# A fused selective-scan layer and mixture-of-experts layer on one core: five activation-table loads a step in place of seven, transposes in one pass, layer-norm statistics of two tiles in one operation, and new orders on four engines

## What is computed

```python
def s6(x):                                   # 32 x 256 x 128 -> the same
    u, o = split(x @ W_in.T)                 # 256 channels each
    u = silu(causal_conv4(u) + conv_b)       # depthwise, 4 taps
    g = u @ W_gate.T                         # 64 delta rows, 16 b, 16 c
    delta = softplus(g[..., :64] @ W_delta.T + delta_bias)
    A = -exp(A_log)                          # 256 channels x 16 states
    # over the positions t:
    h = exp(A * delta[t]) * h + (delta[t] * u[t]) * b[t]
    y[t] = sum_over_states(h * c[t]) + D * u[t]
    return (y * silu(o)) @ W_out.T

def ffn(x):                                  # 8 experts of width 176, the best 2 of them; 1 shared of 352
    scores = softmax(x @ gate_w.T)
    combine = top2(scores) / (sum_of_top2 + 1e-20) * 2.5
    routed = combine-weighted sum of (silu(x @ w_gate[e]) * (x @ w_up[e])) @ w_down[e]
    return routed + (silu(x @ sw_gate) * (x @ sw_up)) @ sw_down

x = x + s6(layernorm(x));  x = x + ffn(layernorm(x))
```

## Time and profile before

| what | value |
|---|---|
| median of three runs | 1169.36 us (1168.85 to 1170.06) |
| the profiled execution, its span | 1170.17 us, 1168.5 us |
| busy: TensorE matmuls, VectorE, ScalarE, GpSimd | 1090.4, 1063.1, 1081.4, 1067.8 us (93, 91, 93, 91%) |
| inject and read on GpSimd | 256 of 2389 ns, 192 of 2388 ns |
| scans on VectorE | 192 of 2284 ns, 64 of 2269 ns |
| decays on ScalarE | 1024 of 463 ns |
| table loads on ScalarE | seven lines of 31 to 35, and nine single ones, 1283 ns each |
| granted TensorE clock | 0.974 over the span |

### The profile page before, as it was taken

The page is one execution under the profiler, slowest core; times in us unless marked ns, Lnnn a source line. Parts: engine busy times, 40 slices in busy tenths (PEclk is TensorE's granted clock), DMA queues, the critical chain, the costliest instruction groups (busy, mean ns, idle before and its releaser), DMA issues.

```text
span 1168.5 us, 25617 instructions
## 1 busy us (share of the span) xinstructions
PE 1090.4 (93%) x9075; PEld 925.3 (79%) x9075; DVE 1063.1 (91%) x1702; ACT 1081.4 (93%) x2182; POOL 1067.8 (91%) x502
## 2 busy tenths in 40 slices
PE   5667999999999999999999999999999999998898
PEld 4435888888888888888888888888888888887687
DVE  5577999999999999999999999999999999998974
ACT  6888999999999999999999999999999999998763
POOL 3699999999999999999999999999999999999930
PEclk9677999999999999999999999999999999998999
DMA  6344444333444433344444334444433344443000
GB/s 173 109 114 110 115 101 102 94 84 107 115 115 101 115 90 88 92 115 114 118 103 101 87 87 111 115 115 102 102 98 85 101 114 115 99 106 99 9 5 10
DMA packets 71481, 115.05 MB, mean 98 GB/s; under 512 B 8173, under 2 KB 30394, under 8 KB 71354
## 3 DMA queue, kind: packets, MB, share of 16 engines
q1 hardware_dynamic: 71354, 113.42, 37.7%
HBM read 41.04 MB, written 5.24 MB: 40 GB/s over the span
## 4 chain that ended last, share of the span: by engine, by line
ACT 60%; issue 14%; POOL 9%; DVE 9%; PE 6%; DMA 1%; ACTq 0%; DVEq 0%; POOLq 0%
ACT decay_ps L538 26%; ACT g_silu L525 5%; DVE decay_ps L758 5%; POOL inject L440 5%; POOL read L454 4%; ACT L655 3%; ACT L642 3%; ACT L638 3%; ACT L692 3%; ACT L668 3%; ACT xn L559 2%; ACT xn L567 2%; DVE features L780 2%; PE acc_ps L1174 2%; ACT L648 2%
## 5 line engine op out<-in xcount | busy, mean ns | idle before, releaser
L440 POOL TENSOR_TENSOR inject<-rep,bc 128x1024 f32<-128x1024 f32 x256 | 605.6, 2389 | 6.3 <-DMA rep<-dd 6.2
L454 POOL TENSOR_TENSOR read<-state,bc 128x1024 f32<-128x1024 f32 x192 | 456.7, 2388 | 29.1 <-DVE state L758 28.9
L758 DVE TENSOR_TENSOR_SCAN state<-decay_ps,inject 128x1024 f32<-128x1024 f32 x192 | 438.6, 2284 | 28.2 <-ACT decay_ps L538 27.3
L538 ACT ACTIVATE decay_ps<-rep,neg_a 128x255 f32<-128x255 f32 x1024 | 425.8, 463 | 2.9 <-DVE state L758 2.5
L1174 PE MATMUL acc_ps<-ffn_down,features 128*128 128x128 f32 (+1 forms) x1792 | 268.3, 279 | 0.4 <-DVE features L788 0.3
L1174 PEld LDWEIGHTS acc_ps<-ffn_down,features 128*128 128x128 f32 (+1 forms) x1792 | 235.1, 191 | 29.6 <-issue 24.9
L1137 PE MATMUL work_ps<-xn2T_part,ffn_gate 128*128 128x256 f32 x1344 | 213.5, 295 | 3.0 <-DVE dd L838 0.7
L1146 PE MATMUL work_ps<-xn2T_part,ffn_up 128*128 128x256 f32 x1344 | 206.7, 293 | 10.1 <-ACT g_silu L525 8.6
L1137 PEld LDWEIGHTS work_ps<-xn2T_part,ffn_gate 128*128 128x128 f32 x1344 | 175.7, 191 | 33.7 <-DVE dd L838 16.5
L1146 PEld LDWEIGHTS work_ps<-xn2T_part,ffn_up 128*128 128x128 f32 x1344 | 172.6, 189 | 33.5 <-ACT xnT_part L579 14.4
L780 DVE TENSOR_TENSOR features<-g_silu,work_ps 128x512 f32<-128x512 f32 x224 | 153.4, 686 | 11.2 <-PE work_ps L1146 10.7
(11 more groups left out here) (143 smaller groups left out, 1316.0 us busy)
## 6 DMA issues: line engine op xcount, KB each, us to landing
rep<-dd SPq DMA_DIRECT2D x256, 256.0 KB, 4.7
bc<-bc_rows SPq DMA_DIRECT2D x64, 512.0 KB, 4.0
x_in<-in_L_attn_x_dram SPq DMA_DIRECT2D x32, 128.0 KB, 2.2
out_dram<-result SPq DMA_DIRECT2D x32, 128.0 KB, 1.8
bc_rows<-g_sb SPq DMA_DIRECT2D x32, 32.0 KB
state<-in_L_ffn_w_gate_dram SPq DMA_DIRECT2D x1, 704.0 KB, 4.3
inject<-in_L_ffn_w_up_dram SPq DMA_DIRECT2D x1, 704.0 KB, 6.0
ffn_down<-in_L_ffn_w_down_dram SPq DMA_DIRECT2D x1, 704.0 KB, 7.5
```

The source lines that it names most:

```text
L440: pool.tensor_tensor(inject[:, slot:slot + many], du_all, b_all, ALU.mult).then_inc(inject_done, many)
L454: pool.tensor_tensor(read[:, slot:slot + many], state[:, first:first + many], c_all, ALU.mult).then_inc(read_done, many)
L538: last = act.activation(decay_ps[:, at % 2, j, 1:T], rep[(HALVES * n + half) % RP][:, j, 0, 1:T], ACT.Exp, scale=neg_a[:, col:col + 1])
L758: dve.tensor_tensor_scan(to, decays, inject[:, at % RI].rearrange("p j t -> p (j t)"), 0.0, ALU.mult, ALU.add).then_inc(state_done, 1)
```

## The change

ScalarE's list is put in another order, with five loads in a step. The exponentials of the router and decays 1 go behind decays 0, into the same table set as before the step's end; norm1 goes from the end of a step to the start of the next, between the silus. The load ahead of the first log_vars now stands at the program's start, and three loads of the prologue go. The two statistics become one bn_stats each, which reads the two tiles alternately (element by element) so that its even and odd halves are the tiles; bn_aggr is dropped, and the log takes the sum of squares with a factor 1/128. The two turns of a normalised tile become transposes. PSUM banks are given out anew, and the orders on GpSimd, VectorE and TensorE change. SP's list stays. The line numbers of the changed program are lower by 3 to 30.

```diff
 
-GATE_BANK = [2, 0, 0, 1, 0, 1, 2]
-UP_BANK = [1, 2, 0, 1, 0, 0, 2]
-
-COMB_BANK = [1, 1, 0, 2, 0, 2]
+GATE_BANK = [2, 0, 0, 1, 0, 1, 1]
+UP_BANK = [1, 2, 1, 2, 0, 2, 1]
+
+COMB_BANK = [0, 1, 0, 2, 1, 0]
 
...
         x_in = [sb(f"x_in{i}", [P, TILES, DIM]) for i in range(RX)]
-        stats1 = sb("stats1", [P, TILES, 6])
-        stats2 = sb("stats2", [P, TILES, 6])
-        mean_var = sb("mean_var", [P, 2 * TILES, 2])
+        stats = sb("stats", [P, 2, 6])
...
+                    act.wait_ge(ln1_var, m + 5)
                 if m >= 0:
-                    act.wait_ge(ln2_var, TILES * (m + 1))
-                act.activation(log_var[:], mean_var[:, :, 1], ACT.Ln, bias=eps[:, 0:1]).then_inc(ln_small, 1)
-                act.activation(neg_mean[:], mean_var[:, :, 0], ACT.Copy, scale=-1.0).then_inc(ln_small, 1)
+                    act.wait_ge(ln2_var, m + 1)
+                act.activation(log_var[:], moments[:, :, 2], ACT.Ln, scale=1.0 / DIM, bias=eps[:, 0:1]).then_inc(ln_small, 1)
+                act.activation(neg_mean[:], moments[:, :, 1], ACT.Copy, scale=-1.0).then_inc(ln_small, 1)
 
             def rstds(m):
...
                 if on(-2):
+                    router_exps(k - 2)
+                if on(-2) or on(1):
                     act.preload_act_table_set("silu_and_others")
+                if on(-2):
                     silu(k - 2, 0)
                     silu(k - 2, 1)
-                if on(-2) or later(0):
-                    act.preload_act_table_set("natural_log_exp_and_others")
-                if on(-2):
-                    router_exps(k - 2)
-                if later(0):
-                    decays(k, 1)
-                if on(-2) or on(1):
-                    act.preload_act_table_set("silu_and_others")
+                if later(2):
+                    norm1(k + 2)
                 if on(-2):
...
                     act.preload_act_table_set("softplus")
-                if on(-2):
-                    act.wait_ge(h_done, PAIRS * (k - 2) + 4)
-                if on(2) and not on(-2):
-                    act.wait_ge(xnT_low, k + 3)
+                if on(-1):
+                    act.wait_ge(x1_done, k)
+                if on(-2) and not on(-1):
+                    act.wait_ge(h_done, PAIRS * (k - 2) + 3)
...
                 if later(2):
                     copy_z(k + 2)
                 if later(1):
                     decays(k + 1, 0)
-
+                    decays(k + 1, 1)
+
+            act.preload_act_table_set("natural_log_exp_and_others")
             log_vars(-4)
             rstds(-4)
-            act.preload_act_table_set("silu_and_others")
             norm1(0)
             xn_high(0)
             xn_low(0)
...
-                dve.wait_ge(ln1_var, TILES * n)
-                for j in range(TILES):
-                    last = dve.bn_stats(stats1[:, j, :], x_in[n % RX][:, j, :])
-                last.then_inc(stats1_done, 1)
-
-            def moments_x(n):
-                dve.wait_ge(stats1_done, n + 1)
                 dve.wait_ge(ln_small, 2 * n)
-                for j in range(TILES):
-                    dve.bn_aggr(mean_var[:, j, :], stats1[:, j, :]).then_inc(ln1_var, 1)
+                dve.bn_stats(stats[:, 0, :], x_in[n % RX][:].rearrange("p j d -> p d j")).then_inc(ln1_var, 1)
 
             def stats_x1(n):
                 dve.wait_ge(x1_done, n + 1)
-                dve.wait_ge(ln2_var, TILES * n)
-                for j in range(TILES):
-                    last = dve.bn_stats(stats2[:, j, :], x1[n % 2][:, j, :])
-                last.then_inc(stats2_done, 1)
-
-            def moments_x1(n):
-                dve.wait_ge(stats2_done, n + 1)
                 dve.wait_ge(ln_small, 2 * (n + 4))
-                for j in range(TILES):
-                    dve.bn_aggr(mean_var[:, TILES + j, :], stats2[:, j, :]).then_inc(ln2_var, 1)
+                dve.bn_stats(stats[:, 1, :], x1[n % 2][:].rearrange("p j d -> p d j")).then_inc(ln2_var, 1)
 
             def add_x1(n):
...
-                if on(-2):
                     gated_up(k - 2, 1)
                 if on(-1):
                     take_y(k - 1, 1)
+                if k == 0:
+                    stats_x(3)
+                if on(-2):
+                    dve.wait_ge(silu_done, PAIRS * (k - 2) + 3)
+                if on(-2) and not on(-2):
+                    dve.wait_ge(silu_done, PAIRS * (k - 2) + 2)
+                if on(-2):
+                    route(k - 2)
                 if on(0):
                     scan(k, 1)
-                if on(1):
-                    dve.wait_ge(gate_done, k + 2)
-                if on(-2) and not on(1):
...
-                                     skip_group_check=True)
+                                     is_transpose=True, skip_group_check=True)
                 last.then_inc(xnT_mm, 1)
 
...
                 if on(1):
                     gate_rows(k + 1)
+                    pe.wait_ge(gate_done, k + 2)
+                if later(2):
+                    turn_xn(k + 2)
                 if on(-1):
                     pe.wait_ge(y_taken, HALVES * (k - 1) + 2)
                 if on(-3):
-                    down(k - 3, 10)
-                if on(-2):
-                    pe.wait_ge(silu_done, PAIRS * (k - 2) + 3)
+                    down(k - 3, 8)
+                    down(k - 3, 9)
...
```

More of the change, by code:

```diff
@@ L941, in body @@
                     read_own_group(k, 4)
-                    take_y(k, 0)
-                    clear_first(k, 4)
                 if on(-2):
@@ L953, in body @@
                 if on(0):
+                    clear_first(k, 4)
+                    take_y(k, 0)
                     scan(k, 5)
@@ L960, in body @@
                     weigh(k - 2, 4)
+                if on(0):
+                    scan(k, 7)
+                if later(4) and k != -1:
+                    stats_x(k + 4)
                 if on(-1):
                     shift_logits(k - 1)
-                if on(0):
-                    scan(k, 7)
+                if on(-2):
+                    weigh(k - 2, 5)
+            dve.wait_ge(prep, PARTS + 2)
             stats_x(0)
-            moments_x(0)
             dve.wait_ge(conv_loaded, 16 * len(conv_loads))
@@ L1215, in body @@
                 if on(-2):
-                    pe.wait_ge(silu_done, PAIRS * (k - 2) + 4)
+                    pe.wait_ge(comb_split, 2 * (k - 2) + 2)
+                if on(-2) and not on(-2):
+                    pe.wait_ge(silu_done, PAIRS * (k - 2) + 3)
+                if on(-2):
+                    turn_comb(k - 2)
                 if later(2):
-                    turn_xn(k + 2)
-                if on(-3):
-                    down(k - 3, 13)
+                    turn_rest_xn(k + 2)
                 if on(-2):
@@ L1225, in body @@
                 if on(-3):
+                    down(k - 3, 13)
+                if on(2):
+                    pe.wait_ge(xnT_low, k + 3)
+                if on(-2):
+                    ups(k - 2, 3)
+                if on(-3):
                     pe.wait_ge(result_done, k - 2)
@@ L1296, in body @@
                 if on(-2):
-                    spread_comb(k - 2, 3)
+                    ups(k - 2, 6)
+                    down(k - 2, 1)
+                    down(k - 2, 2)
                 if on(0):
@@ L1300, in body @@
                 if on(-2):
-                    down(k - 2, 4)
+                    pe.wait_ge(hc_done, COMBS * (k - 2) + 4)
+                if on(-1):
+                    turn_xn2(k - 1)
+                if on(-2):
+                    down(k - 2, 3)
+                    pe.wait_ge(h_done, PAIRS * (k - 2) + 7)
+                    spread_comb(k - 2, 4)
                 if on(-1):
```

197 lines of the change are left out of this document (78 added, 119 removed).

## The result

The changed kernel takes 1162.05 us (median of 4 runs, 1160.76 to 1162.3) against 1169.71 us before (1168.85 to 1170.18). The ratio is 0.9933, 95% interval 0.9916 to 0.995: faster by 7.7 us, where 27.7 were forecast and 1158 was the upper end of the range. The profiled execution took 1162.3 us, its span is 1160.6 us, so 1.7 us lie outside it as before.

What follows compares the result with a forecast made beforehand. GpSimd's 33.02 us of work was taken to bound the new step, ScalarE's loop the old one. Steady 20.3, prologue 3.4 and emptying 4.0, together 27.7 us off 1170.17, gave 1142 after the median adjustment; range 1136 to 1158.

Steps and rivals of the forecast that it cites:

- the one-pass turns: Four 128x128 products a step on TensorE made transposes: 0.5 us less work, nothing of it on the steady path.
- The gate loop: Gate to decays 2 beside VectorE's work, 4.6 us each; as rival bound: step 33.4, 1151 us; gate or other loop 0.19.
- The last rival: The change does nothing to the step; the ends alone give 7.4 us, 1162; step hardly shorter: chance 0.08.
- the ends: Prologue and emptying, outside the 31 steady steps: together 7.4 us less.
- The steady term: 31 steps falling from 33.755 to 33.10 us each: 20.3 us less.
- GpSimd's 33.02 us: GpSimd's own work in a step, back to back, untouched by the change: the floor that would bound the step.
- The loads: Two table loads a step less on ScalarE, 2.57 us; hidden once GpSimd bounds, so worth at most 0.735 us per step.
- The statistics: One bn_stats over both tiles on VectorE, no bn_aggr: 0.34 us each, VectorE's work 0.45 us less per step.
- The filling: The prologue, with fewer table loads on ScalarE's path and an earlier first turn: 3.4 us less, ends 1.4 and 5.
- The emptying: Behind the last step: reads following each other, 0.8 us, and loads on ScalarE, about 3.2: 4.0 us less.

Runs made afterwards that it cites:

- e2: The changed kernel with its two turns of a normalised tile as ordinary four-pass float32 products again: 1169.13 us, ratio 0.9992.
- e3: The kernel before with only the two turns made one-pass transposes: 1168.45 us, ratio 0.999.
- e4: The changed kernel with two more table loads a step on ScalarE, between silu 1 and norm 1, so seven again: 1221.16 us, ratio 1.044.
- e5: The changed kernel with TensorE's down chunk 4, between up 3 and gate_rows, cut to one 8 by 8 product (output incomplete): 1157.61 us, ratio 0.9901.
- e7: The changed kernel with decays 2 on ScalarE made of three exponentials instead of four from the second group on (part stale): 1155.29 us, ratio 0.9881.
- e10: The changed kernel with each of VectorE's two bn_stats a step issued twice, first into a spare tile: 1160.16 us, ratio 0.9923.
- e1: The changed kernel with TensorE's wait for the gate's silu and turn_xn moved behind down 8 and 9: 1161.1 us, ratio 0.9926.
- e13: The changed kernel with down chunks 1 to 13 of the last pair but one made for the first tile only (output wrong): 1159.3 us, ratio 0.9913.
- e9: e1 with, in addition, copy_combT and xn_low ahead of decays 3 on ScalarE, against the changed kernel: 1167.25 us, ratio 0.998.

## Why the prediction was wrong

- **The failed step** is the sentence on the one-pass turns: TensorE's "real work is under 32.6 us. It is not the bound; nothing of this is on the path in the steady step". I subtracted drains from its busy time, but a group's drain lies under the start of the next group (527.19 + 0.97 is past 528.01), and busy time counts such a moment once: in the step of 33.56 us TensorE is shown idle for 0.78 us, and 0.69 of them are its one listed wait. From up 4 to gate_rows it is packed for 20.51 of 33.57 us. The turn in that stretch, which the prediction put at nothing, is worth 0.26 us a step (e2), and in the old order next to nothing (e3).
- **The gate loop** was seen, but only against VectorE (4.6 against 4.6 us). Its other end is TensorE: gate_rows, then ScalarE to xn_low for up 3 and to silu 4 for up 4, 13.06 us, then TensorE's 20.51 back to gate_rows. 13.06 + 20.51 = 33.57 is the step. e4, e5 and e7 change one of the two parts each, and the step follows. The rival of this name, with 33.4 and 1151, was near in the step, but its other end was VectorE, and its sign, a scan that waits over 0.3 us for decays 2, is absent: scan 2 starts 0.03 us behind them. The last rival, that the change does nothing to the step, gave 1162, and that it meets the measured time is luck: it had all 7.4 us from the ends, which gave 0.9, and nothing from the steps, which gave 7.0.
- **The steady term**: forecast 20.3 us, measured 7.0. GpSimd's 33.02 us was never reached; the lowest step, e7's, is 33.36. The 13.3 us that are missing here are the larger part of the miss. With the ends as forecast the time would have been 1155, inside the range; it took the emptying to leave it.
- **The loads**: two of 1.28 us are gone in each step, and ScalarE's busy time fell by 2.18 us. Their worth was hidden not by GpSimd, as I wrote, but by the order: e4 and the kernel before differ by 1.4 us a step at seven loads each.
- **The statistics**: 0.34 us forecast, 0.32 and 0.35 measured. Off the path (e10).
- **The filling**: 2.5 us for 3.4 forecast. The first group-5 read lies at 63.3 to 64.6 us in the thirteen other profiles of the changed kernel and its variants, and at 66.3 in e3, the only other one with the old prologue. The first convolution's 24 products alone take 4.98 us in the kernel after and 3.92 in e1. So one profile of each kernel does not settle this term, and 3.4 is not contradicted.
- **The emptying**: forecast 4.0 us less, measured 1.6 more. The last three reads do not follow each other: the second and third wait 0.99 and 0.40 us for scans. I counted ScalarE's loads there, and TensorE's work is on the path in part (e13). Up 1, gates 2, down 8 and 9 now stand behind the last states instead of ahead of them. That this is the 1.6 us I only argue; it was not undone alone, and the cause stays open.
- **Slips in the working** that change nothing: 31 x 0.735 is 22.8, not 23.0, and the rows that stand within 1.3 us of the step are those of four engines, not five.

## What to carry to other kernels

Write the loop of a step as its stretches from handoff to handoff, engine by engine. They always add up to the step; what has to be checked is that each is filled with work, for instance by the distance between the same two groups in another run (0.70 us here, 0.36 in e9). A saving counts only if it lies in one of them. A new order is a change of its own: price it with the old amount of work before you subtract what is saved. When cutting 0.4 us moves the step by 0.17, look for the next chain that ends there; moving work between ties costs as easily as it gains.
